# Keys turned to token layout by VectorE block transposes and SBUF transfers, not by TensorE

## The reference, cut to what matters

```python
q = jax.nn.elu(q * E ** (-0.5)) + EPS_FEAT
k = jax.nn.elu(k) + EPS_FEAT
def step(carry, qkv_t):
    kv_s, k_s = carry
    q_t, k_t, v_t = qkv_t
    kv_s = kv_s + jnp.einsum('bhe,bhf->bhef', k_t, v_t)
    k_s = k_s + k_t
    num = jnp.einsum('bhe,bhef->bhf', q_t, kv_s)
    den = jnp.einsum('bhe,bhe->bh', q_t, k_s)[..., None] + EPS_DEN
    return ((kv_s, k_s), num / den)
```

## Time and profile before

| what | value |
|---|---|
| three runs | 2020.95, 2022.31, 2024.04 us; median 2022.31 us |
| the profiled execution | 2021.64 us, its span 2019.9 us |
| TensorE busy | 1987.5 us, 98% of the span |
| VectorE busy | 1415.2 us, 70% |
| ScalarE busy | 937.0 us, 46% |
| GpSimd busy | 864.1 us, 43% |

### The profile page before, as it was taken

One profiled execution on the slowest core, in us unless ns is written; L12 is line 12 of the kernel. 1 busy time (PEld: TensorE's weight loads), 2 busy tenths in 40 slices (PEclk: granted clock), 3 DMA queues, 4 the chain that ended last, 5 costly groups with the idle time before them and its releaser, 6 DMA issues. The chain is left out here.

```text
span 2019.9 us, 43984 instructions
## 1 busy us (share of the span) xinstructions
PE 1987.5 (98%) x16260; PEld 1620.6 (80%) x16260; DVE 1415.2 (70%) x2346; ACT 937.0 (46%) x1605; POOL 864.1 (43%) x718
## 2 busy tenths in 40 slices
PE   7999999999999999999999999999999999999999
PEld 4788888888888888888778888888888888888887
DVE  7876887777887777886785757747576475765743
ACT  5444444344444444444363536435364353644533
POOL 2533443344443344443424443444434444444444
PEclk9999999999999999999999999999999999999999
DMA  7112222233222232122275564655546565465553
GB/s 265 43 54 69 71 84 90 90 100 95 64 90 90 90 101 95 59 95 64 86 297 183 180 195 147 228 167 191 197 143 218 185 197 178 149 224 167 168 170 105
DMA packets 157163, 276.79 MB, mean 137 GB/s; under 512 B 11105, under 2 KB 35681, under 8 KB 157026
## 3 DMA queue, kind: packets, MB, share of 16 engines
q1 hardware_dynamic: 156498, 273.73, 41.2%
q10 hardware_dynamic: 528, 1.05, 0.1%
HBM read 208.67 MB, written 66.06 MB: 136 GB/s over the span
## 5 line engine op out<-in xcount | busy, mean ns | idle before, releaser
L1471 POOL TENSOR_TENSOR h_lo<-y_rows,h_hi 128x512 fp32r<-128x512 f32 x192 | 246.6, 1303 | 366.5 <-ACT h_hi L1569 366.4
L433 POOL TENSOR_TENSOR x_res<-y,x_res 128x512 f32<-128x512 f32 x64 | 83.2, 1300 | 319.1 <-DVE y L847 308.6
L584 ACT ACTIVATE z_exp<-pj,qk_neg 128x512 f32<-128x512 f32 x128 | 88.0, 687 | 175.6 <-PE pj L1097 172.4
L826 DVE TENSOR_TENSOR probs<-sc,causal 128x512 f32<-128x512 f32 x256 | 158.5, 679 | 12.2 <-PE sc L1117 12.1
L1097 PE MATMUL pj<-xt_hi,w_hi 128*128 128x512 f32 x512 | 146.1, 407 | 5.8 <-DVE a_t L836 5.2
L1899 PE MATMUL sc<-wd,h_hi 128*128 128x512 f32 x384 | 150.6, 392 | 0.0
L1899 PE MATMUL sc<-wd,h_lo 128*128 128x512 f32 x384 | 149.7, 390 | 0.0
L422 POOL TENSOR_TENSOR a_lo<-a_t,a_hi 128x512 fp32r<-128x512 f32 x60 | 78.0, 1300 | 164.4 <-ACT a_hi L603 164.4
L1097 PE MATMUL pj<-xt_lo,w_hi 128*128 128x512 f32 x512 | 138.1, 391 | 1.7 <-DVE xt_lo L773 1.7
L1097 PE MATMUL pj<-xt_hi,w_lo 128*128 128x512 f32 x512 | 138.2, 392 | 0.0
L1684 DVE TENSOR_TENSOR r_den<-pj,k_tok 128x512 f32<-128x512 f32 x96 | 66.2, 690 | 97.9 <-ACT k_tok L1552 55.8
(11 more groups left out here) (250 smaller groups left out, 5451.4 us busy)
## 6 DMA issues: line engine op xcount, KB each, us to landing
w_hi<-parts SPq DMA_DIRECT2D x48, 1024.0 KB, 5.2
w_lo<-parts SPq DMA_DIRECT2D x48, 1024.0 KB, 5.2
x_mid<-x_res SPq DMA_DIRECT2D x96, 256.0 KB, 2.7
x_res<-in_L_attn_x SPq DMA_DIRECT2D x64, 256.0 KB, 2.8
xg<-in_L_attn_x SPq DMA_DIRECT2D x15, 1024.0 KB, 6.9
x_res<-x_mid SPq DMA_DIRECT2D x60, 256.0 KB, 4.0
full<-x_mid SPq DMA_DIRECT2D x60, 256.0 KB, 3.6
parts<-r_den SPq DMA_DIRECT2D x48, 256.0 KB, 2.3
```

The costliest lines, as they stand in the source:

```text
L433: pool.tensor_tensor(out=x_res[:, slot, :], in0=y[:, :], in1=x_res[:, slot, :], op=ALU.add).then_inc(y_ready, 1)
L584: act.activation(z_exp[:, n % 2, :], pj[:, n % 2, :], ACT.Relu, bias=qk_neg[:, 1 - kind, c:c + 1], scale=-scale).then_inc(below_ready, 1)
L826: dve.tensor_tensor(out=probs[:, h, :].rearrange("p (c i) -> p c i", c=C), in0=sc[:, h, :].rearrange("p (c i) -> p c i", c=C), in1=causal[ ...
L1471: pool.tensor_tensor(out=h_lo[b], in0=h[i], in1=h_hi[b].bitcast(F32), op=ALU.subtract).then_inc(h_lo_ready, 1)
```

## The change

TensorE no longer turns keys. For each tile VectorE makes one 32x32 block transpose of `kt` into `k_block` (`k_blocks`, 128x512). A block transpose leaves each block in its own 32 partitions, so SP then issues 16 transfers of 32 partitions by 128 elements (16 KB), SBUF to SBUF, that put each block row where the token layout wants it (`move_k`). There are two `k_tok` buffers, used in turn; the second is a part of `r_den[1]` that nothing else uses then. `add_state` waits for the transfers (`k_moved`) and reads its 32 key columns at a new place in the row. `k_turn` on TensorE, `k_rows` on ScalarE, and the waits on them are gone.

```diff
+MOVE = 16 * HPC * HPC
...
-    k_tok = sbuf(s, "k_tok", [P, D])
+    k_tok = [sbuf(s, "k_tok", [P, D]), r_den[1][:, 0, :]]
...
+        def move_k(g, t):
+
+            tile = g * GT + t
+            wait(sp, kblock_ready, tile + 1)
+            if isinstance(tile, int) and tile < 2:
+                sp.wait_ge(*((late_mm, 2), (o_lo, C))[tile])
+            for b in range(P // E):
+                for h in range(HPC):
+                    sp.dma_start(k_tok[t % 2][b * E:(b + 1) * E, h * P:(h + 1) * P],
+                                 k_block[h * E:(h + 1) * E, b * P:(b + 1) * P]).then_inc(k_moved[t % 2], 16)
...
+        move_k(0, 0)
+
         def group(g, parity):
...
                 load_residual(tile, t % 2, g * 2 + t // 2)
+                if not isinstance(g, int) or tile + 2 < NG * GT:
+                    move_k(*((g, t + 1) if t + 1 < GT else (g + 1, 0)))
...
-        def k_rows(tile):
-            wait(act, kt_ps, tile + 1)
-            wait(act, state_ready, tile)
-            act.activation(k_tok[:, :], turn_bank_of(tile), ACT.Copy).then_inc(ktok_ready, 1)
...
+        def k_blocks(g, parity, t):
+
+            tile = g * GT + t
+            wait(dve, phi_ready, g * 2 * C + 2 * C - 1)
+            wait(dve, state_ready, tile - 1)
+            wait(dve, k_moved[(t + 1) % 2], MOVE * (g * 2 + (t + 1) // 2))
+            dve.transpose(k_block[:, :].rearrange("p (b c e) -> p c b e", b=P // E, c=C),
+                          kt[parity][:, :, t * P:(t + 1) * P].rearrange("p c (b i) -> p c b i", i=E)).then_inc(kblock_ready, 1)
...
             wait(pe, y_gated, min(tile - 1, (NG - 1) * GT - 1) if isinstance(tile, int) else tile - 1)
-            wait(pe, ktok_ready, tile)
...
-        def k_turn(tile, parity, t):
...
-            for c in range(C):
-                mm = pe.transpose(turn_bank_of(tile)[:, c * P:(c + 1) * P], kt[parity][:, c, t * P:(t + 1) * P], ident[:, :])
-            mm.then_inc(kt_ps, 1)
...
             elif t < 3:
-                pe.wait_ge(ktok_ready, tile + 1)
+                pe.wait_ge(v_ready, NG * C - 1)
...
-        def add_state(tile, parity, t):
-            wait(pe, ktok_ready, tile + 1)
+        def add_state(g, parity, t):
+            wait(pe, k_moved[t % 2], MOVE * (g * 2 + t // 2 + 1))
             for c in range(C):
                 for h in range(HPC):
                     f = slice(c * P + h * E, c * P + (h + 1) * E)
-                    mm = pe.matmul(state[h * E:(h + 1) * E, f], k_tok[:, f], v[parity][:, t, f],
+                    kf = slice(h * P + c * E, h * P + (c + 1) * E)
+                    mm = pe.matmul(state[h * E:(h + 1) * E, f], k_tok[t % 2][:, kf], v[parity][:, t, f],
```

More of the change, by code:

```diff
@@ L42 @@
 Programs = namedtuple("Programs", "sync gpsimd scalar vector tensor")
-Signals = namedtuple("Signals", "wide_ready wd_in xt_ps xf_ready a_ready y_gated y_ready y_out xr_ready state_ready ktok_ready op_ready pj_ready part_out b_ready sum_made b_high")
+Signals = namedtuple("Signals", "wide_ready wd_in xt_ps xf_ready a_ready y_gated y_ready y_out xr_ready state_ready op_ready pj_ready part_out b_ready sum_made b_high")
 Shared = namedtuple("Shared", "xg xf h_hi h_lo ring b_hi b_lo full wd silu_sum saved gate h y x_res gb_row pairs sums dn")
-Turned = namedtuple("Turned", "kt qt v r_den probs prod k_sum a_hi a_lo")
+Turned = namedtuple("Turned", "kt qt v r_den probs prod k_block k_sum a_hi a_lo")
 Later = namedtuple("Later", "wd h_hi h_lo y_rows full")
+MOVE = 16 * HPC * HPC
 def wait(eng, sem, value):
@@ L109, in build @@
         prod = sbuf(top, "prod", [P, 2, GN])
-        sbuf(top, "unused_row", [P, GN])
+        k_block = sbuf(top, "k_block", [P, GN])
         k_sum = sbuf(top, "k_sum", [P, 2, GN])
@@ L114, in build @@
         r_den[0] = sbuf(top, "r_den0", [P, C, GN])
-        turned = Turned(kt, qt, v, r_den, probs, prod, k_sum, a_hi, a_lo)
+        turned = Turned(kt, qt, v, r_den, probs, prod, k_block, k_sum, a_hi, a_lo)
         later = Later(wd, h_hi, h_lo, y_rows, full)
@@ L188, in attention @@
     z_relu = sbuf(s, "z_relu", [P, 2, GN])
-    kt, qt, v, r_den, probs, prod, k_sum, a_hi, a_lo = turned
+    kt, qt, v, r_den, probs, prod, k_block, k_sum, a_hi, a_lo = turned
     xf = sbuf(s, "xf", [P, 2, GN])
@@ L232, in attention @@
     num_ready, a_ready, a_hi_ready, a_lo_ready = sem("num_ready"), sem("a_ready"), sem("a_hi_ready"), sem("a_lo_ready")
-    kt_ps, ktok_ready, state_ready, kv_ready = sem("kt_ps"), sem("ktok_ready"), sem("state_ready"), sem("kv_ready")
+    kblock_ready, k_moved, state_ready, kv_ready = sem("kblock_ready"), [sem(f"k_moved{i}") for i in range(2)], sem("state_ready"), sem("kv_ready")
     op_ready, y_gated, xr_ready, y_ready = sem("op_ready"), sem("y_gated"), sem("xr_ready"), sem("y_ready")
@@ L258, in attention @@
                     (blocks, filled), b_hi, b_lo, x_full, [later.wd[:, j, :] for j in range(HB)],
-                    [r_den[0][:, 2, :], r_den[0][:, 3, :], bv_row[:, :]], [k_tok[:, :], flat_diag],
+                    [r_den[0][:, 2, :], r_den[0][:, 3, :], bv_row[:, :]], [k_tok[0][:, :], flat_diag],
                     [k_sum[:, 1, :], gabo_row[:, :]], [later.y_rows[:, i, :] for i in range(2)], [a_t[:, :], y[:, :]],
@@ L269, in attention @@
     late_bank = tuple(sc[:, i, :] for i in range(2))
-    c_bc = k_tok[:, :].rearrange("p (k n) -> p k n", k=C)
+    c_bc = k_tok[0][:, :].rearrange("p (k n) -> p k n", k=C)
     silu_row, junk = a_t, y
@@ L664, in ahead_of_last @@
             exp_relu(n, 1)
-            k_rows(g * GT)
             state_out(g * GT)
@@ L671, in ahead_of_last @@
             exp_relu(n, 4)
-            k_rows(g * GT + 1)
             state_out(g * GT + 1)
@@ L686, in ahead_of_last @@
             xt_full(g + 2, 1, x_bank)
-            k_rows(g * GT + 2)
             xt_high(g + 2, parity, 1)
@@ L700, in ahead_of_last @@
                 act.wait_ge(made_out[1], g * 16 + (-16))
-            k_rows(g * GT + 3)
             xt_high(g + 2, parity, 3)
@@ L921, in vector @@
         feature(0, 0, 6)
+        k_blocks(0, 0, 0)
         dve.wait_ge(bv_in, 16)
@@ L949, in ahead_of_last @@
             feature(n, other, 1)
+            k_blocks(g, parity, 1)
             gate_last(g, 0)
@@ L962, in ahead_of_last @@
             spread(g * GT + 1, g, parity, 1)
+            k_blocks(g, parity, 2)
             den_of(n, 0)
@@ L975, in ahead_of_last @@
             spread(g * GT + 2, g, parity, 2)
+            k_blocks(g, parity, 3)
             feature(n, other, 5)
@@ L990, in ahead_of_last @@
             spread(g * GT + 3, g, parity, 3)
+            k_blocks(n, other, 0)
             den_of(n, 3)
@@ L1236, in rest @@
             ahead = not isinstance(g, int) or g + 1 < NG
-            if not ahead and t + 1 < GT:
-                k_turn(tile, parity, t)
             if not isinstance(tile, int) or tile > 0:
@@ L1242, in rest @@
                 x_turn(g + 2, 2 * t - 3, x_bank)
-            if ahead:
-                k_turn(tile, parity, t)
             if isinstance(tile, int) and tile == (NG - 2) * GT:
@@ L1254, in rest @@
             if ahead:
-                add_state(tile, parity, t)
+                add_state(g, parity, t)
             if not ahead and t + 1 < GT:
-                add_state(tile, parity, t)
+                add_state(g, parity, t)
         def group(g, parity):
@@ L1291, in tensor @@
         return last_group, last_projection
-    signals = Signals(wide_ready, wd_in, xt_ps, xf_ready, a_ready, y_gated, y_ready, y_out, xr_ready, state_ready, ktok_ready, op_ready,
+    signals = Signals(wide_ready, wd_in, xt_ps, xf_ready, a_ready, y_gated, y_ready, y_out, xr_ready, state_ready, op_ready,
                       pj_ready, part_out + made_out, b_ready, sum_made, b_high)
```

## The result

| | before | after |
|---|---|---|
| median (lowest to highest), us | 2022.62 (2020.95 to 2024.04) | 2083.37 (2079.67 to 2084.29) |
| span of the profiled execution, us | 2019.9 | 2081.5 |

The ratio is 1.0297, 95% interval 1.0279 to 1.0315: 61 us slower, where 20 us faster was forecast, and above the range's upper end of 2030.

What follows compares the result with a forecast made beforehand. The attention was taken as a queue of TensorE work, busy 98% of the span. Savings of 15.8 + 3.5 + 0.9 less 0.6 lost made 19.6 us, from 2021.64 to a forecast of 2002 us, range 1992 to 2030.

Steps and rivals of the forecast that it cites:

- What goes, on TensorE: Key transposes leave TensorE: 0.44 us a stage saved, except stage 1 of most loop groups, where the divide wait grows.
- Rivals 1 and 4: 1: all stages save 0.53 us, 1990, chance 0.09. 4: nothing gained, handover or key wait costs the time, 2022, 0.11.
- What comes, on VectorE: One block transpose a tile, 0.64 us to the next start, hidden by VectorE's idle time in the loop's stages.
- Rival 3: VectorE becomes the bound everywhere: 0.2 us more a tile, 63 tiles, 13 us, 2034; chance 0.04.
- What comes, on SP: Sixteen issues a tile at 0.47 us each (0.37 to 0.71), landing 2.0 to 2.3 us, in time for the next transpose.
- rival 2: Transfers set the pace, stalling VectorE's next transpose: gain gone at 0.62 us an issue, 2038 at 0.71; slower, chance 0.13.
- The stated sign of failure: On SP: the prediction is wrong if the new issues stand 0.6 us apart.
- What waits behind SP: Stores and residual loads behind SP's sixteen issues, each up to 7 us later; counted as nothing.
- The last group: Nothing saved on TensorE; tile 62's block transpose delays `gate_y`: 0.6 us lost, 3 us as the far end.

Runs made afterwards that it cites:

- eight moves: The changed kernel with 8 of its 16 transfers a tile, the other 8 left out, so half the keys are not moved: 2003.2 us.
- the one over DRAM with all keys moved: The changed kernel with the 16 transfers replaced by one store of `k_block` to DRAM and four loads back: 2004.4 us.
- the run with VectorE's part alone: The kernel before, plus VectorE's 63 block transposes whose result nobody reads, no transfers, TensorE still turning keys: 2032.5 us.
- the kernels with four or eight moves: The changed kernel with only 4 or 8 of its 16 transfers a tile: 2004.7 us with four, 2003.2 us with eight.
- the run in four forms: The kernel before plus sixteen unawaited 16 KB transfers a tile, differing by tile in partitions and in SBUF or DRAM ends: 2034.3 us, run once.
- without it (32): The kernel before plus sixteen 16 KB SBUF to SBUF transfers a tile that wait for no transpose and nobody awaits: 2054.2 us.
- with `xg` on time: The changed kernel with all 16 transfers, `xg` from group 2 on loaded by ScalarE's queue instead of SP's: 2059.2 us.
- the run with two queues: The changed kernel with eight of each tile's sixteen moves issued by ScalarE, the very first tile's all staying on SP: 2160.8 us.

## Why the prediction was wrong, and where it was right

**What goes, on TensorE: right.** Busy time fell by 28.8 us with eight moves (1987.5 to 1958.7); forecast 28. The wait for the divide became 11.7 us, forecast 10.5. Two groups of that kernel, from one issue of `xg` at 487.80 us to that at 607.02, take 59.6 us each; forecast 59.6. The kernels in which the queue keeps up, the one over DRAM with all keys moved among them, stand at 2003.2 to 2004.7; the forecast was 2002.0. Rivals 1 and 4, all saved and nothing saved, fall with that.

**What comes, on VectorE: right in size.** The line of after, beside the earlier trace rows:

```profile
L835 DVE STREAM_TRANSPOSE k_block<-kt x63: 657/700/715, 64.2 to 1049.4; 128x512 f32<-128x512 f32 x63
```

It is hidden once TensorE's transposes go. Rival 3's 13 us are near the 10.5 of the run with VectorE's part alone, but by chance: it is another wait than it named, and they do not add up with the rest in the kernels with four or eight moves.

**What comes, on SP: the first step that failed.** "For 16 KB I take 0.47: nearest in size." The rows it came from have an end in DRAM. With both ends in SBUF it measured 0.60 (four) to 0.74 (sixteen). The upper bound, 0.71, taken from twelve loads of 256 KB, happened to be the better value; that is luck, as those have an end in DRAM too. "No row shows this kind of transfer" stands in rival 2, and the value was yet taken for the nearest size, where the run in four forms, all of one size, shows that the ends make the difference. The stated sign of failure ("if the issues stand 0.6 us apart") is what the trace shows.

**What waits behind SP: the second step that failed.** "A residual is needed over a stage after its load, and I count nothing." The prediction named stores and residual loads and passed over `xg`, which is behind them in the same queue. For the residuals it was right in the loop: GpSimd waits for them in the last group alone (18.2 us, 3 times). The margin of `xg` was in the trace of before, SP's and VectorE's timeline:

```profile
496.37 0.38 SPq L301 DMA_DIRECT2D xg<-in_L_attn_x  x1
```

```profile
506.02 1.87 DVE L741 BATCH_NORM_STATS2 stats<-xg 128x6 f32<-128x512 f32 x3
```

```profile
DMA to landing us min/median/max: 5.4/6.9/8.1
```

Issued 9.65 us before its use and 6.9 us on its way at the median: 2.75 us of margin, in a queue to which each stage adds 7 us even by the forecast's 0.47. In after the landing of `xg` is 7.0 us, so the transfer is no slower; it is issued too late. (Residual loads do land later, 4.3 us for 2.8.) Eight moves (5 to 6 us a tile) can still be taken up by the queue's idle time, which before was most of a group. Sixteen cannot, with SP's wait for VectorE (61 us lost) or without it (32). This step is a share and not the whole: with `xg` on time the kernel still takes 2059. Both shares go back to the first step, the time that sixteen issues hold the queue.

**Rival 2: the right resource, one victim of two.** It had the transfers set the pace and a price of 2038 at 0.71 us an issue, through the next block transpose alone. Its threshold for a loss, 0.62 us, was passed, and the wait that it describes came: 12.1 us up to 260 us of after's span. From there on each stall of VectorE also delays SP's next sixteen, `xg` is late (52.6 us), and of the other wait 2.0 us are left up to 950 us. 2083 was out of its reach, since it priced each group's delay once and at one place; with `xg` on time, what is left stands at 2059, and TensorE is busy 17 us longer in it than with eight moves (1975.6 against 1958.7). By its own formula 0.53 and 0.58 us an issue give 2003 and 2013, not 2005 and 2016; nothing hangs on that.

**The last group.** Counted at 0.6 us, with 3 as the far end. TensorE's wait for keys is 7.9 us there, and it ran slower behind it.

**The clock** was in no step: it is most of the 25.6 us of longer busy time, out of the 80 us above the kernel with eight moves.

## What to carry to other kernels

Price what an in-order queue already carries before putting more into it: for every load behind the new work, its margin is use minus issue minus landing, and the smallest margin decides, also for a tile that the change does not touch. Take the price of an issue from a row whose ends lie in the same memories, and if there is none, work the dear end of its range through everything that stands in the queue. If the issuing engine waits for an engine that waits for its loads, a delay can come back each round; here fewer and larger transfers, even over DRAM, took the queue out of the loop.

## What the runs showed of the hardware that was not expected

- Issues on SP in a row, 16 KB each: with both ends in SBUF 0.60 to 0.74 us apiece (0.58 to 0.60 at the median), for 32, 64 or 128 partitions; with one end in DRAM 0.46 to 0.53 (0.42 at the median). Alone, a store of 256 KB was 0.33 us.
- In the run with two queues ScalarE started no activation while it issued eight transfers: 4.6 to 4.7 us of standstill.
- A bounce over DRAM (256 KB out, 4 times 64 KB back) took 2.3 and 2.0 us to land at the median, no slower each than the 2.3 us of the store in the earlier trace rows.
- After waits of 2.98 and 7.88 us TensorE was at its lower clock level for a while: 1.91 us for matmuls of 1.07, and 2.09 for matmuls of 1.17.
- VectorE stood still for some 2 us ten times when nothing but its own block transposes was added; in each an 8 KB packet came on the instruction queue. That this is the cause was not tried.
